# SyncE copies eight sequences' cache blocks into one table during the scan, and each of them then needs one set of gathers instead of two

## The reference, cut to what matters

```python
w = cond_weights[conditions]                     # per sequence
u = einsum('bct,bcd->bdt', x, w)                 # conditioned input of the scan
x = x + selective_scan(u, delta, A, B, C, D)     # h = exp(delta*A)*h + delta*u*B ; y = C.h + u*D, 16 states
# attention with a paged cache of keys and values, 4 key heads, 8 query heads, 64 wide
q, k, v = x Wq, x Wk, x Wv ; q, k = rms, rotary at pos = kv_len + 0..63
k_blocks = k_blocks.at[blk, :, off, :].set(k)    # the new rows are written into the cache ...
v_blocks = v_blocks.at[blk, :, off, :].set(v)
k_all = k_blocks[block_tables]                   # ... and then each sequence reads its blocks,
v_all = v_blocks[block_tables]                   #     which may be blocks another sequence wrote
p = softmax(where(in the last 256 positions, q k_all, -inf)) ; a = (p v_all) Wo
# feed-forward on the better half of every 64 tokens
scores = a . w_r ; idx = top_k(scores, half) ; out[idx] = gelu(a[idx] w1 + b1) w2 + b2
x = x + out
```

## Time and profile before

| what | us |
|---|---|
| median of 3 runs (lowest, highest) | 1834.98 (1834.75, 1838.16) |
| the profiled execution, whole | 1836.52 |
| its span, first to last instruction | 1834.7 |
| TensorE busy in it | 1622.8 (88%) |
| VectorE busy | 1443.4 (79%) |
| ScalarE busy | 1279.6 (70%) |
| GpSimd busy | 1254.5 (68%) |

### The profile page before, as it was taken

How to read it: one execution, slowest core, us unless ns; L and a number is a source line. 1 busy time by engine, 2 the same in 40 slices (tenths; PEclk the granted TensorE clock), 3 DMA queues, 4 the chain that set the end, 5 groups by cost and what they waited for, 6 DMA issues and landing times.

```text
span 1834.7 us, 30427 instructions
## 1 busy us (share of the span) xinstructions
PE 1622.8 (88%) x9591; PEld 1127.9 (61%) x9591; DVE 1443.4 (79%) x2542; ACT 1279.6 (70%) x4011; POOL 1254.5 (68%) x1136
## 2 busy tenths in 40 slices
PE   6788888888888888877877899999999999999999
PEld 6666565566666656655545575756657575665755
DVE  8999999999999999999967674655656565574522
ACT  6888888888888888876566674756657465564622
POOL 5789999999999999999777764446454445641010
PEclk9999999999999999998978999999999999999999
DMA  6434344344334435433366663334343334431010
GB/s 232 162 139 167 110 164 169 121 150 169 132 134 175 155 111 175 154 110 117 103 203 196 194 181 96 89 93 127 89 111 95 83 98 112 114 89 42 19 35 12
DMA packets 130039, 230.44 MB, mean 126 GB/s; under 512 B 31496, under 2 KB 82716, under 8 KB 124504
## 3 DMA queue, kind: packets, MB, share of 16 engines
q1 hardware_dynamic: 94456, 158.50, 25.3%
q0 software_dynamic: 35424, 70.00, 14.5%
HBM read 212.88 MB, written 43.65 MB: 140 GB/s over the span
## 4 chain that ended last, share of the span: by engine, by line
PE 40%; issue 5%; POOL 4%; ACT 3%; DVE 3%; DMA 1%; SPq 0%; DVEq 0%; ACTq 0%; POOLq 0%
PE attn_psum L2087 12%; PE attn_psum L2103 12%; PE attn_psum L2022 4%; PE attn_psum L2035 4%; PE attn_psum L2015 4%; PE attn_psum L2006 2%; DVE hid L1070 1%; POOL kv_at L1607 1%; POOL kv_at L1599 1%; ACT xh L1745 1%; POOL hid L560 1%; ACT th L1746 1%; PE attn_psum L2047 1%; PE attn_psum L1996 1%; DMA kv_at<-kv_scratch,idx_new 1%
## 5 line engine op out<-in xcount | busy, mean ns | idle before, releaser
L1169 DVE TENSOR_TENSOR_SCAN hid<-scan_psum,hid 128x1024 f32<-128x1024 f32 x256 | 580.7, 2269 | 0.0
L1394 PE MATMUL scan_psum<-ident,hid 128*128 128x128 f32 x2048 | 342.4, 286 | 121.5 <-POOL hid L560 118.9
L1394 PEld LDWEIGHTS scan_psum<-ident,hid 128*128 128x128 f32 x2048 | 254.9, 146 | 281.0 <-POOL hid L560 153.2
L560 POOL TENSOR_TENSOR hid<-hid,kv_at 128x1024 f32<-128x1024 f32 x128 | 306.4, 2407 | 23.7 <-DVE hid L1169 22.9
L560 POOL TENSOR_TENSOR hid<-hid,bc 128x1024 f32<-128x1024 f32 x128 | 305.9, 2403 | 17.6 <-DVE hid L1169 17.2
L1852 DVE CUSTOM_DVE_ANT_0 prob<-attn_psum,mask 128x336 f32<-128x336 f32 x256 | 119.8, 504 | 237.6 <-PE attn_psum L2015 237.4
L1714 ACT COPY p_t<-attn_psum 112x384 f32<-112x384 f32 x256 | 122.4, 485 | 227.9 <-PE attn_psum L2022 227.8
L1599 POOL DMA_INDIRECT kv_at<-in_kv_rows,idx_old x183 | 175.6, 960 | 105.8 <-PE attn_psum L2035 54.9
L2103 PE MATMUL attn_psum<-w,ffn_hid 128*128 128x512 f32 x512 | 237.9, 595 | 4.9 <-DVE y_sb L1928 4.9
L2087 PE MATMUL attn_psum<-xs_in,w 128*128 128x256 f32 x1024 | 232.7, 381 | 7.8 <-ACT xs_in L1720 6.6
L1607 POOL DMA_INDIRECT kv_at<-kv_scratch,idx_new x189 | 197.9, 1047 | 60.4 <-issue 54.9
(11 more groups left out here) (231 smaller groups left out, 3019.5 us busy)
## 6 DMA issues: line engine op xcount, KB each, us to landing
bc<-bc_scratch SPq DMA_DIRECT2D x16, 2048.0 KB, 10.2
kv_at<-bc_scratch SPq DMA_DIRECT2D x15, 2048.0 KB, 10.0
q_scratch<-qg SPq DMA_DIRECT2D x32, 260.0 KB, 2.1
early<-q_scratch SPq DMA_DIRECT2D x32, 260.0 KB
x_pair<-in_x_pairs SPq DMA_DIRECT2D x32, 256.0 KB, 4.5
f_wo<-in_w_o SPq DMA_DIRECT2D x32, 256.0 KB, 3.3
out_t<-x_rows SPq DMA_DIRECT2D x64, 128.0 KB, 2.9
a_scratch<-a_sb SPq DMA_DIRECT2D x32, 256.0 KB
```

Of the source, the lines that this page charges most:

```text
L560: pool.tensor_tensor(hid[:, r, :, :], hid[:, r, :, :], bc[q // 2][:, 4 * j:4 * j + 4, 1, :], ALU.mult).then_inc(pool_hc, 1)
L1169: nc.vector.tensor_tensor_scan(states, decay[k % 2], states, 0.0, ALU.mult, ALU.add).then_inc(dve_h, 1)
L1394: mm = nc.tensor.matmul(yc[g], hid[:, e % RING, i, P * g:P * g + P], ident[:], start=False, stop=(k % 4 == 3 and i == 3), is_transpose=Tru ...
```

## The change

The scratch table of new rows becomes the lower part of a larger one, `row_scratch`: its first 8 x 336 rows are a place for the blocks of the first eight sequences, and the new rows follow. During the scan, from s = 2 to s = 29, SyncE at the end of every quarter reads six block numbers from SBUF into a register and copies the block of each (16 rows, 32 KB) from `kv_rows` to its place, 168 copies in all. VectorE makes a third table `idx_row`, which for the first eight sequences names either the copied row or the new row. Each of these then takes three gathers, from `row_scratch`. NKV1 goes from 3 to 8; the gathers in the scan go. The stores of the last two groups are split in values and keys, and the load of the second pair's queries moves behind the keys.

```diff
-NKV1 = 3
+NKV1 = 8
+NSTAGE = NKV1 * NKEY
...
@@ SyncE, quarter @@
                     sp.dma_start(S["sin"], sin[:]).then_inc(st_rope, 16)
-                if isinstance(t, int) and t == NT and q < 2:
-                    attention_first(q)
+                if s == 2:
+                    sp.wait_ge(ld_found, 32)
+                if 2 <= s < 2 + NSLOT * NKV1 // 6:
+                    for n in range(6 * (s - 2), 6 * (s - 2) + 6):
+                        stage(n)
+                if isinstance(t, int) and t == NT and q == 0:
+                    attention_first()
+                if isinstance(t, int) and t == NT and q == 1:
+                    store_values()
                 if isinstance(t, int) and t == NT and q == 2:
                     store_last()
...
+            def store_values():
+                sp.wait_ge(act_lc, 3)
+                for i in range(2):
+                    g = NG - 2 + i
+                    sp.dma_start(S["kv_new"][g * GRP:g * GRP + GRP, G * HD:KV], last_kv[:, i, G * HD:KV]
+                                 ).then_inc(st_kv[g % 2], 16)
+
             def store_last():
-                sp.wait_ge(act_lc, 3)
                 sp.wait_ge(dve_lk, 2)
                 for i in range(2):
-                    store_keys(NG - 2 + i, last_kv[:, i, :])
+                    g = NG - 2 + i
+                    sp.dma_start(S["kv_new"][g * GRP:g * GRP + GRP, 0:G * HD], last_kv[:, i, 0:G * HD]
+                                 ).then_inc(st_kv[g % 2], 16)
+                attention_second()
...
+            def stage(n):
+
+                b, i = n // NSLOT, n % NSLOT
+                block = sp.value_load(found_i[b:b + 1, i:i + 1], min_val=0, max_val=NROW // BLOCK - 1)
+                sp.dma_start(S["rows"][NKEY * b + BLOCK * i:NKEY * b + BLOCK * i + BLOCK, :],
+                             A["kv_rows"][bass.ds(block * BLOCK, BLOCK), :]).then_inc(st_stage, 16)
...
@@ GpSimd, end of the first block @@
             def gather_first_new(b):
 
                 for i in range(2):
-                    pool.wait_ge(st_kv[i], 16 * NG // 2)
-                pool.wait_ge(ld_old[b], 16 * NKC)
+                    pool.wait_ge(st_kv[i], 16 * (NG // 2 + 1))
+                pool.wait_ge(st_stage, 16 * NSLOT * NKV1)
                 for c in range(NKC):
-                    pool.indirect_dma_start(kv_tile(kv_at, b)[:, c, :], None, S["kv_new"],
-                                            bass.IndirectOffsetOnAxis(ap=idx_new[:, c, b:b + 1], axis=0),
-                                            bounds_check=NTOK - 1, oob_is_err=False).then_inc(ld_kv[b], 16)
+                    pool.indirect_dma_start(kv_tile(kv_at, b)[:, c, :], None, S["rows"],
+                                            bass.IndirectOffsetOnAxis(ap=idx_row[:, c, b:b + 1], axis=0)
+                                            ).then_inc(ld_kv[b], 16)
...
@@ VectorE, last_writers @@
-                chained(v.tensor_scalar(far, winner, 0.5, FAR, ALU.is_lt, ALU.mult))
-                v.scalar_tensor_tensor(idx_new[:].rearrange("p c b -> p (c b)"), winner, -1.0, far, ALU.add, ALU.add
-                                       ).then_inc(idx_ok, 1)
+                writer = winner.rearrange("p (c b) -> p c b", c=NKC)[:, :, 0:NKV1]
+                mark(v.tensor_scalar(far, winner, 0.5, FAR, ALU.is_lt, ALU.mult))
+                chained(v.scalar_tensor_tensor(moved, writer, float(NSTAGE - 1), staged, ALU.add, ALU.subtract))
+                chained(v.scalar_tensor_tensor(moved, writer, 0.5, moved, ALU.is_ge, ALU.mult))
+                v.scalar_tensor_tensor(idx_new[:].rearrange("p c b -> p (c b)"), winner, float(NSTAGE - 1), far,
+                                       ALU.add, ALU.add).then_inc(idx_ok, 1)
+                v.tensor_tensor(idx_row[:], moved, staged, ALU.add).then_inc(idx_ok, 1)
...
@@ GpSimd, attention block @@
+            def gather_first(s):
+
+                for c in range(NKC):
+                    pool.indirect_dma_start(kv[s][:, c, :], None, S["rows"],
+                                            bass.IndirectOffsetOnAxis(ap=idx_row[:, c, s:s + 1], axis=0)
+                                            ).then_inc(ld_kv[s], 16)
...
             def gather(i, s):
 
                 gather_old(NKV * i + s, s)
                 if s:
                     gather_new(i, s - 1)
-                else:
+                elif i > 1:
                     gather_new(i - 1, NKV - 1)
...
-                    if i == 1 and s == 7:
+                    if i == 1 and s == 6:
                         gather_rows(0, 1)
...
-            for s in range(NKV2, NKV - 1):
-                gather_new(0, s)
-                if s + NKV1 - NKV2 < NKV:
-                    gather_old(s + NKV1 - NKV2, s + NKV1 - NKV2)
+            for s in range(NKV2, NKV1):
+                gather_first(s)
             eight(1)
```

More of the change, by code:

```diff
@@ L46 @@
 NINT = 2 + B + 2 * NG
[L47 removed]
+NSHEET = 4 + NWC * BLOCK + NCH * (2 + NST) + HALF + 2 * HD + NKC * NKV1
 SEL = T // 2
@@ L68, in constants @@
     out, at = [], 0
-    for n in (NWC * BLOCK, 1, 1, 1, 1, NCH, NCH, NCH * NST, HALF, 2 * HD):
+    for n in (NWC * BLOCK, 1, 1, 1, 1, NCH, NCH, NCH * NST, HALF, 2 * HD, NKC * NKV1):
         out.append(sheet[:, at:at + n])
@@ L205, in scan_block @@
         far = lay(small[3], 0, NKC * B)[0:KC]
+        moved = lay(small[3], NKC * B, NKC, NKV1)[0:KC]
+        staged = staged[0:KC].rearrange("p (c b) -> p c b", c=NKC)
         win_rows = lay(small[2], 0, NSLOT * BLOCK)[0:B]
@@ L442, in attention_first, with attention_second @@
                 sp.dma_start(rope[k][:, 1, :], S["sin"][:, k * HALF:k * HALF + HALF]).then_inc(ld_q[k], 16)
+            def attention_first():
+                q_scale, dist, q_in, rope = early_tiles(early)
+                sp.wait_ge(st_rope, 32)
+                sp.wait_ge(pe_res, NCH * (2 * NT - 1))
+                load_queries(0)
+                sp.dma_start(dist, A["dist"]).then_inc(a_const, 16)
+                sp.wait_ge(pe_q, NG - 2)
+                sp.wait_ge(pe_kv, NG - 2)
+                for i in range(2):
+                    sp.dma_start(q_scale[:, i, :], A["q_scale2"][i].partition_broadcast(P)).then_inc(a_const, 16)
+            def attention_second():
+                load_queries(1)
             for dst, src, landed in ((ints, A["ints"], s_ints), (sheet, A["sheet"], s_sheet),
@@ L1486, in attention_ffn_block @@
         early_half_ok = sem("early_half")
-        ld_old, ld_q, ld_kv = W["ld_old"], W["ld_q"], W["ld_kv"]
+        ld_q, ld_kv = W["ld_q"], W["ld_kv"]
+        ld_old = [sem(f"ld_old{i}") for i in range(NKV)]
         st_a = [sem(f"st_a{i}") for i in range(2)]
@@ L2159, in program @@
     S["q"] = nc.dram_tensor("q_scratch", [NTOK, QW], F32).ap()
-    S["kv_new"] = nc.dram_tensor("kv_scratch", [NTOK, KV], F32).ap()
+    S["rows"] = nc.dram_tensor("row_scratch", [NSTAGE + NTOK, KV], F32).ap()
+    S["kv_new"] = S["rows"][NSTAGE:NSTAGE + NTOK, :]
     S["cos"] = nc.dram_tensor("cos_scratch", [P, NG * HALF], F32).ap()
@@ L2178, in program @@
         W["ld_kv"] = [ctx.enter_context(nc.semaphore(f"ld_kv{i}")) for i in range(NKV)]
-        W["ld_old"] = [ctx.enter_context(nc.semaphore(f"ld_old{i}")) for i in range(NKV)]
         W["ld_q"] = [ctx.enter_context(nc.semaphore(f"ld_q{i}")) for i in range(2)]
```

54 lines of the change are left out of this document (13 added, 41 removed).

## The result

The changed kernel takes 1890.74 us (median of 4 runs, 1889.48 to 1896.26) against 1836.02 us for the kernel before in the same comparison: a ratio of 1.030, 95% interval 1.0283 to 1.0317, 55 us slower. The forecast was 1883 us, slower. The execution in the profile took 1896.26 us (span 1894.5), the longest of the four, so the trace shows 5.5 us more loss than the median.

A forecast was written before the change was run, and what follows sets the result against it. VectorE's gapless chain bounds the scan; TensorE bounds the attention, with air only from 926 to 1040 us. 1836.5 + 57 + 0.8 - 9 = 1885, forecast as 1883 us against the median; range 1824 to 1945.

The forecast's parts named there:

- 6X: SyncE's delay per quarter from six copies, each costing X for block-number read, small instructions and issue: forecast 7.3 us.
- 6X - 3.25: Scan: us lost per two quarters while the keys do not wait for ScalarE; 14 times that gives 57 us.
- the second formula: Scan, keys waiting for ScalarE: a quarter lasts 19.6 + 6X us, longer than 27.1 only if 6X exceeds 7.5.
- The cost of a copy: SyncE's time for one copy in the scan: 1.22 us, of which 0.75 for the read with small instructions.
- The room of 3.25 us per two quarters: Scan: how much later SyncE can be before VectorE stops, 1.65 us at ScalarE's copy plus 1.60 at the exponentials.
- Cheap copies: Rival, scan: X up to 0.64, read hidden under the previous copy's issue, attention's gain decides; some 1827 us, chance 0.20.
- Dear copies: Rival, scan: X over 1.8, a read of more than 1.3 us; 1953 us, at the bound 2015; chance 0.14.
- A store that overtakes: Rival, scan: the rows' store lands ahead of earlier transfers, so ScalarE never waits; 1827 us, chance 0.04.
- The rival in which the attention gains nothing: Attention: 3 x 229 KB per sequence beside weight loads land as late as before; 9 us more, 1892 us, chance 0.05.
- VectorE at the start: Three more operations on 24 elements between two scans, straight on the path: 0.8 us, bounds 0.4 and 1.2.
- The hand-over: From scan to attention: keys stored 0.5 us earlier but first gathers bring all 112 rows; 0, bounds 1.5 either way.
- The attention: Fewer gathers for sequences 1 to 7 shorten TensorE's waits for rows: 9 us gained of 12.8, at most 15.

The follow-up runs named there:

- experiment 1: The changed kernel with all 168 copies moved behind the rows' store in SyncE's queue: 1829.78 us, ratio 0.9964 to the kernel before.
- experiment 2: The changed kernel, copies in place, rows' stores counted by quarter parity so ScalarE's copy waits for the store of two quarters ago: 1829.64 us, ratio 0.9965.
- e3_twice: The changed kernel with each block number read twice: 1948.23 us, ratio 1.0614 to the kernel before.
- experiment 4: The kernel before with only SyncE's 168 copies added, into a table nobody reads: 1902.69 us, ratio 1.0357.
- e2_const: The changed kernel with block numbers constant, so no register read and output not the reference's: 1839.28 us, ratio 1.0019 to the kernel before.
- experiment 5: The changed kernel with the 512 KB load of x issued behind the rows' store instead of ahead: 1873.83 us, ratio 1.0198 to the kernel before.
- experiment 6: The kernel before with only the last values stored apart from and ahead of the keys, second pair's queries behind them: 1835.9 us, ratio 0.9994.
- experiment 7: The kernel of experiment 1 with the router's first rows gathered later, before sequences 13 and 15: 1825.27 us, ratio 0.9936 to the kernel before.

## Why the prediction was right

**The mechanism** held: the copies delay everything behind them in SyncE's queue, the rows' store lands behind broadcast and x, ScalarE's copy and the exponentials wait for it, then VectorE. Experiments 1 and 2 take the delay and the wait away in turn, and each removes the whole loss.

**One link was different, and the sum did not feel it.** The prediction had the keys' store of a late quarter come on time, as long as the keys do not wait for ScalarE. In the odd quarters of the changed kernel they do: their store follows ScalarE's copy by 5.56 us (495.26 to 500.82), where it was 10.9 before (459.55 to 470.47). So of the 5.2 us lost there the keys lose 1.5 too, and the next quarter gets some 3.75 us more room and not 5.2. With its own 2.75 + 1.60 this is 8.1 us, enough for 6X = 7.79, so the even quarters lose nothing. At 6X = 11.41 they lose 3.3 us by this working (3.1 on average in the trace of e3_twice), the odd ones that much less than 6X - 3.25, and two together again 6X - 3.25. Only when the even ones lose over 3.75 us, at a 6X of some 11.85, would the second formula take over.

**The cost of a copy** was 1.22 us in the sum and 1.30 measured: 0.47 for the issue (0.49 measured) and 0.75 for the read with what belongs to it, of which the read is 0.27 and the rest small instructions and gaps. No row of before showed a read, so the 0.75 was a choice between bounds of 0.47 and 2.37 us for the whole, which would have given 1827 to 2015 us. That it fell so near is in part luck; the formula around it is not.

**The room of 3.25 us per two quarters** measures 3.0 to 3.4 in the table, 3.1 in experiment 4. With 6X = 7.79 instead of 7.3 the step "14 x (6X - 3.25)" gives 64 us, where 57 stood and 61.4 (changed kernel) and 65.4 (copies alone) were measured. The single odd quarter shown above looks like less room (7.64 - 5.19 = 2.45 us), but there the two quarters are 5.3 us longer and the mean is lower. One quarter is no measure of the sum.

**The rivals.** Cheap copies (6X below 3.9): e2_const has 6X = 3.79 and loses 9.5 us, where the prediction's formula gives 7.6. Dear copies: the second formula (6X - 7.5 in every quarter) would give 109 us at 6X = 11.41, the first 114; 118.5 were measured, so the times cannot tell the two apart there. A store that overtakes: excluded, since it landed behind x in the changed kernel and moved when x moved (experiment 5). The Trainium skill (DMA: Bandwidth & Descriptors, Queues, rings and completion order) says that completion is not first in, first out per issuing engine, but also that the signal of a transfer lands only after every earlier write of the same DMA engine. The traces agree with the second half: the 128 KB take 11 us behind 2.5 MB issued just before, and up to 2.9 us in the even quarter of before, where the broadcast ahead (issued at 473.38, 10.0 us to landing) has only 2 us left to go.

The rival in which the attention gains nothing is excluded too, by the gain of 6.7 us in experiment 1, although a gather from the new table takes 8.1 us to land (median) where one of new rows took 3.3 before.

**The signs.** ScalarE's copy waits for the store in 26 quarters, of both kinds, and up to 7.6 us, not only in those with x and up to 4. A quarter is 29.7 us on average ("about 29"), the last scan comes 69.6 us later in the trace ("some 57"), the copies are 1.3 us apart ("1.2"), and behind the first one TensorE's waits for gathers are 3.7 us ("about 4").

**VectorE at the start**: 0.8 us in the sum. The gap between scan and next product grew from 0.64 to 1.04 us (one operation 0.36, the three new ones 0.17 to 0.18 each and overlapping): 0.4 us, the lower bound.

**The hand-over** was put at 0. From the last scan's end to TensorE's first key it was 27.5 us and is 25.4, a gain of 2.1 in the trace; the stores' share of it is the 1.1 us of experiment 6, within the bound of 1.5 and within noise.

**The attention**: 9 us in the sum. With the loss gone, all edits together gain 6.7 us (experiment 1, interval 4.4 to 8.8); with the loss in place, copies alone against the changed kernel, 65.4 - 54.7 = 10.7. The mechanism was that of the prediction: GpSimd stood 10.6 us for the router's numbers, and one later sequence came 1.7 us late. What it under-rated is the price of this standing. Gathering the router's rows later gave 4.5 us (1829.78 to 1825.27; 5.3 with each one's own runs of before), more than the one wait of 2.0 us that the trace of experiment 1 shows; the mean clock of TensorE from 926 to 1040 us was 0.90 there and is 0.94 in experiment 7.

**The sum**: 57 + 0.8 - 9 gave 49, and 55 were measured. X accounts for +7 of the difference and the room for -2; the rest is 1.5 less gain. Where the 4 us between 6.7 and 10.7 of the attention's gain come from was not settled.

## What to carry to other kernels

An engine's idle time is free only where nothing behind it in its own queue has a deadline: six copies just ahead of a quarter's loads cost 61 us in all, and with the same six a few lines further on VectorE waits for nothing. So before placing work in a queue, find the transfer behind it with the least room, here a 128 KB store behind a 2 MB load, and who waits for it. Then ask whether that wait is needed: this one guarded columns that the store did not touch, and counting the stores by parity took the queue off the path.

## What the runs showed of the hardware

- A read of one number from SBUF into a register of SyncE took 0.27 us, with its register instructions and gaps 0.67 us; a copy of 32 KB from memory to memory took 0.49 us to issue and 2.0 us to land.
- Issuing one and the same pair of stores took SyncE 0.94 us in most quarters of the kernel before (up to 3.46 near the end of the scan) and 2.59 us in the changed one, right behind broadcast and x. It was 0.94 again right behind a broadcast alone (experiment 2, at 483.30), but 2.50 behind a broadcast with x issued only afterwards (experiment 5). So neither the broadcast alone nor x ahead explains it, and the cause stays open.
- VectorE's scans are slightly longer in the changed kernel, 2.283 instead of 2.269 us, 3.8 us over 256 of them. The kernel of experiment 1, with the same copies, has 2.274, and so has that of experiment 6, without any: that the traffic of the copies is the cause is not shown.

```profile
L1169 DVE TENSOR_TENSOR_SCAN hid<-scan_psum,hid 128x1024 f32<-128x1024 f32 x256 | 580.7, 2269 | 0.0
```

```profile
L1180 DVE TENSOR_TENSOR_SCAN hid<-scan_psum,hid 128x1024 f32<-128x1024 f32 x256 | 584.5, 2283 | 66.4 <-ACT scan_psum L729 66.4
```

The first row is of the page of before, the second of after.
